# The last layer of a graph network: slice sums over normalized rows, and its weights loaded beside ELU

## The reference, cut to what matters

```python
# x: [1, 3125, 256] normalized rows; H = 8 heads, D = 64, G = 64 slices
fx_mid = (x @ W_fx + b_fx).reshape(B, N, H, D).transpose(0, 2, 1, 3)
x_mid = (x @ W_x + b_x).reshape(B, N, H, D).transpose(0, 2, 1, 3)
slice_weights = softmax((x_mid @ W_slice + b_slice) / clip(temperature, 0.1, 5.0), axis=-1)
slice_norm = slice_weights.sum(axis=2)
slice_token = einsum('bhnc,bhng->bhgc', fx_mid, slice_weights) / (slice_norm[..., None] + 1e-05)
q, k, v = slice_token @ W_q, slice_token @ W_k, slice_token @ W_v
attn = softmax(einsum('bhgc,bhkc->bhgk', q, k) * D ** -0.5, axis=-1)
out_slice = einsum('bhgk,bhkc->bhgc', attn, v)
out_x = einsum('bhgc,bhng->bhnc', out_slice, slice_weights)
return out_x.transpose(0, 2, 1, 3).reshape(B, N, 512) @ W_out + b_out
```

## Time and profile before

| | |
|---|---|
| median of 3 runs | 5513.17 us (5511.9 to 5520.0) |
| the profiled execution's own time | 5524.19 us |
| its span, first to last instruction | 5522.4 us |
| busy: PE, PEld | 4435.7 us (80%), 2884.0 us (52%) |
| busy: DVE, ACT, POOL | 3479.8 (63%), 2302.5 (42%), 3326.5 us (60%) |
| mean granted TensorE clock | 0.853 of full speed |

### The profile page before, as it was taken

How to read it: one execution, slowest core, us unless ns; L and a number is a source line. 1 busy time by engine, 2 the same in 40 slices (tenths; PEclk the granted TensorE clock), 3 DMA queues, 4 the chain that set the end, 5 groups by cost and what they waited for, 6 DMA issues and landing times. The chain is left out here.

```text
span 5522.4 us, 88485 instructions
## 1 busy us (share of the span) xinstructions
PE 4435.7 (80%) x20192; PEld 2884.0 (52%) x20192; DVE 3479.8 (63%) x12187; ACT 2302.5 (42%) x7944; POOL 3326.5 (60%) x3594
## 2 busy tenths in 40 slices
PE   6977777999867778487699968888597688878868
PEld 4533336899723335344455546666495333336536
DVE  8977884311267774624555558888524688878875
ACT  6900552333333334122555545554143455545521
POOL 7777775666477773352377747766024477758710
PEclk8966998999856668556999979999698799999978
DMA  2543346788567772132444458887475488877600
GB/s 68 161 140 104 105 103 211 251 298 292 181 187 206 206 205 40 55 104 73 116 129 130 129 133 280 281 265 207 136 212 142 118 230 232 231 209 232 182 19 24
DMA packets 528344, 914.80 MB, mean 166 GB/s; under 512 B 95861, under 2 KB 378436, under 8 KB 519396
## 3 DMA queue, kind: packets, MB, share of 16 engines
q0 software_dynamic: 154432, 449.76, 29.2%
q1 hardware_dynamic: 312974, 330.74, 19.2%
q10 hardware_dynamic: 60438, 128.64, 7.5%
HBM read 739.18 MB, written 169.60 MB: 165 GB/s over the span
## 5 line engine op out<-in xcount | busy, mean ns | idle before, releaser
L1212 PE MATMUL bank<-small 128*125 128x256 f32 x1660 | 733.8, 555 | 286.9 <-DVE small L1175 172.2
L1156 POOL DMA_INDIRECT small<-tabA,idxD x830 | 804.0, 969 | 263.9 <-issue 144.8
L1212 PEld LDWEIGHTS bank<-small 128*125 128x125 f32 x1660 | 336.4, 251 | 680.7 <-issue 361.8
L2629 POOL DMA_INDIRECT big<-tabT,edge x415 | 404.0, 973 | 247.8 <-SPq L200 121.6
L3165 POOL DMA_INDIRECT small<-tabC,idxD x415 | 408.6, 985 | 185.7 <-DVEq L202 59.4
L2903 POOL DMA_INDIRECT big<-tabB,idxD x415 | 400.2, 964 | 178.6 <-issue 86.3
L1745 DVE COPY small<-bank 128x256 f32<-128x256 f32 x176 | 74.8, 425 | 675.3 <-PE bank L1800 675.3
L1066 POOL DMA_INDIRECT eaS<-edge,rowE x391 | 393.0, 1005 | 164.7 <-issue 114.3
L1713 POOL DMA_INDIRECT small<-tabA,small x176 | 168.9, 960 | 455.5 <-SPq L200 196.5
L1187 DVE TENSOR_TENSOR big<-big,bank 125x256 f32 x830 | 346.1, 417 | 145.4 <-PE bank L1212 122.9
L3243 PE MATMUL bank<-big,cst 128*125 128x512 f32 x830 | 426.3, 595 | 0.5 <-ACT big L3230 0.5
(11 more groups left out here) (530 smaller groups left out, 10902.8 us busy)
## 6 DMA issues: line engine op xcount, KB each, us to landing
big<-in_L_w ACTq DMA_DIRECT2D x56, 1024.0 KB
small<-eaS SPq DMA_DIRECT2D x415, 128.0 KB
eaS<-small SPq DMA_DIRECT2D x415, 128.0 KB, 3.6
big<-eaS SPq DMA_DIRECT2D x415, 128.0 KB, 3.6
edge<-in_ea SPq DMA_DIRECT2D x390, 128.0 KB
big<-in_L2f_w ACTq DMA_DIRECT2D x64, 512.0 KB
big<-rowsD SPq DMA_DIRECT2D x104, 256.0 KB, 4.1
ytab<-small ACTq DMA_DIRECT2D x176, 128.0 KB
```

The lines of the kernel that those rows point to most:

```text
L1156: g.indirect_dma_start(out=self.gb[k % self.RG], out_offset=None, in_=K.tabA, in_offset=row_index(K.idxD, k)).then_inc(*self.got.up(k))
L1212: p.matmul(self.K.bank[k % 4][0:PT, 0:D], self.oh[k % self.RO][:, 0:PT], self.gb[k % self.RG], start=True, stop=True).then_inc(*self.summe ...
L2629: g.indirect_dma_start(out=self.rows(k)[:, 0, :], out_offset=None, in_=K.tabT, in_offset=row_index(K.idxS, k)).then_inc(*self.got.up(k))
```

## The change

The values are not computed tile by tile any more. PE adds the product of normalized rows (transposed by being the weights of the matmul) and slice weights over all tiles, in two banks of 128 features x 512 (head, slice) pairs. POOL adds the slice weights themselves into one tile. Behind the loop one matmul with ones sums that tile over its partitions (the norm), and 24 small ones multiply the sums with W_fx and the bias with the summed weights, which gives the tokens already transposed. DVE divides by the norm in that form, so it inverts 64 x 512 numbers. The loop's buffers change with it: the normalized rows get a ring of 7, the logits three banks, the transposes two banks.

The weight loads move in SP's order, and the fold in PE's, from behind the meeting after the ELU to before it.

```diff
+    RX = 7
...
+        self.weight, self.nr = W(512), W(512)
+        self.sums = [W(512) for _ in range(2)]
...
-    def sync(self, s):
+    def weights_sync(self, s):
...                                      (the twelve loads, as before)
+    def sync(self, s):
+        K = self.K
         K.meet(s, "s")
         K.meet(s, "s")
...
     def gpsimd(self, g):
+        w = self.weight[0:PT, :]
+        for t in range(T):
+            g.wait_ge(*self.soft.n(t + 1))
+            sv = self.sw[0:PT, t * 512:(t + 1) * 512]
+            if t == 0:
+                g.tensor_copy(w, sv).then_inc(*self.weighed.up)
+            else:
+                g.wait_ge(*self.weighed.n(t))
+                g.tensor_tensor(w, w, sv, ALU.add).then_inc(*self.weighed.up)
         self.K.meet(g, "g")
         self.K.meet(g, "g")
 
-    def tensor(self, p):
+    def fold(self, p):
...                                      (the 24 small matmuls, as before)
+    def tensor(self, p):
...
-        p.wait_ge(*self.one.n(1))
...
-                for q in range(4):
-                    m = p.matmul(K.bank[4 + q][:, 0:129], self.sw[0:PT, t * 512 + q * 128:t * 512 + (q + 1) * 128],
-                                 self.fx[t % 4][0:PT, q * 129:(q + 1) * 129], start=(t == 0), stop=(t == T - 1))
+                for c in range(2):
+                    m = p.matmul(K.bank[4 + c][:, :], self.xn[t % self.RX][0:PT, c * 128:(c + 1) * 128],
+                                 self.sw[0:PT, t * 512:(t + 1) * 512], start=(t == 0), stop=(t == T - 1))
...
-                    m = p.matmul(K.bank[1 + t % 2][0:PT, :], xT[:, c, :], self.wc[:, c * 512:(c + 1) * 512], start=(c == 0), stop=(c == 1))
+                    m = p.matmul(K.bank[1 + t % 3][0:PT, :], xT[:, c, :], self.wc[:, c * 512:(c + 1) * 512], start=(c == 0), stop=(c == 1))
                 m.then_inc(*self.logits.up)
-                if t:
-                    p.wait_ge(*self.copied.n(t))
-                for c in range(2):
-                    m = p.matmul(K.bank[3][0:PT, :], xT[:, c, :], self.wf[:, c * 512:(c + 1) * 512], start=(c == 0), stop=(c == 1))
-                m.then_inc(*self.values.up)
...
         K.meet(p, "p")
-        p.wait_ge(*self.means.n(1))
-        for q in range(4):
-            m = p.transpose(K.bank[0][0:64, q * 128:(q + 1) * 128], self.tok[:, q * 64:(q + 1) * 64], K.ident)
-        m.then_inc(*self.means_t.up)
+        p.wait_ge(*self.weighed.all)
+        p.matmul(K.bank[6][0:64, :], K.ones[0:PT, 0:64], self.weight[0:PT, :], start=True, stop=True).then_inc(*self.norm.up)
+        p.wait_ge(*self.kept_a.n(1))
+        p.wait_ge(*self.kept_v.n(1))
+        for h in range(8):
+            at = slice(h * 64, (h + 1) * 64)
+            p.matmul(K.bank[0][0:64, at], self.bf[0:PT, at], self.weight[0:PT, at], start=True, stop=False)
+            for c in range(2):
+                m = p.matmul(K.bank[0][0:64, at], self.wf[:, c * 512 + h * 64:c * 512 + h * 64 + 64], self.sums[c][:, at], start=False, stop=(c == 1))
+        m.then_inc(*self.folded_t.up)
...                                      (scalar)
         K.meet(a, "a")
+        a.activation(self.sums[0], K.bank[4][:, :], ACT.Copy).then_inc(*self.kept_a.up)
...                                      (vector)
-        for f in self.fx:
-            ins = v.memset(f.rearrange("p (q c) -> p q c", c=129)[:, :, 128:129], 1.0)
-        ins.then_inc(*self.one.up)
...
-                v.wait_ge(*self.values.n(t + 1))
-                if t >= 4:
-                    v.wait_ge(*self.slot.n(t - 3))
-                v.tensor_tensor(self.fx[t % 4][0:PT, :].rearrange("p (q c) -> p q c", c=129)[:, :, 0:128],
-                                K.bank[3][0:PT, :].rearrange("p (q c) -> p q c", c=128),
-                                self.bf[0:PT, :].rearrange("p (q c) -> p q c", c=128), ALU.add).then_inc(*self.copied.up)
...
-                if i >= 2:
-                    v.wait_ge(*self.flipped.n(i - 1))
-                ln_apply(K, v, i, self.xn[i % 2][0:PT, :]).then_inc(*self.normed.up)
+                if i >= self.RX:
+                    v.wait_ge(*self.slot.n(i - self.RX + 1))
+                ln_apply(K, v, i, self.xn[i % self.RX][0:PT, :]).then_inc(*self.normed.up)
         K.meet(v, "v")
...                                      (the division of four banks by their norm goes)
+        nr = self.nr[0:64, :]
+        v.tensor_copy(self.sums[1], K.bank[5][:, :]).then_inc(*self.kept_v.up)
+        v.wait_ge(*self.norm.n(1))
+        v.tensor_scalar(nr, K.bank[6][0:64, :], 1e-5, None, ALU.add).then_inc(*own.up)
+        v.wait_ge(*own.all)
+        v.reciprocal(nr, nr).then_inc(*self.inverse.up)
+        v.wait_ge(*self.inverse.n(1))
+        v.wait_ge(*self.folded_t.n(1))
+        v.tensor_tensor(self.tT[0:64, :], K.bank[0][0:64, :], nr, ALU.mult).then_inc(*self.tokens.up)
...                                      (tensor and sync of the whole program)
             K.meet(p, "p")
+            l3_ffn.fold(p)
             K.meet(p, "p")
             l3_ffn.tensor(p)
...
             K.meet(s, "s")
+            l3_ffn.weights_sync(s)
             K.meet(s, "s")
             l3_ffn.sync(s)
```

More of the change, by code:

```diff
@@ L3498, in __init__ @@
         keep = K.w_at
-        self.xn, self.xT = [g(D) for _ in range(2)], [g(256) for _ in range(2)]
-        self.lgt, self.fx = [g(512) for _ in range(2)], [g(4 * 129) for _ in range(4)]
+        self.xn, self.xT = [g(D) for _ in range(self.RX)], [g(256) for _ in range(2)]
+        self.lgt = [g(512) for _ in range(2)]
         self.mx, self.sm = [g(8) for _ in range(2)], [g(8) for _ in range(2)]
-        self.one = K.mark(1)
-        (self.normed, self.flipped, self.turned, self.logits, self.values, self.taken, self.copied, self.shifted, self.expo,
-         self.soft, self.slot) = (K.mark(T) for _ in range(11))
+        (self.normed, self.flipped, self.turned, self.logits, self.taken, self.shifted, self.expo,
+         self.soft, self.slot, self.weighed) = (K.mark(T) for _ in range(10))
         K.close()
         K.w_at, K.g_at = keep, 0
-        self.tok, self.nr = g(4 * 64), g(4)
         self.tT, self.qT, self.kT, self.vv, self.at, self.aT, self.oT = (g(512) for _ in range(7))
@@ L3510, in __init__ @@
         self.Bm = W(4 * D)
-        (self.means, self.means_t, self.tokens, self.qm, self.km, self.vm, self.qkv, self.scores, self.ready, self.expa, self.attn,
-         self.attn_t, self.attn_c, self.mixed, self.mixed_c) = (K.mark(1) for _ in range(15))
+        (self.norm, self.inverse, self.kept_a, self.kept_v, self.folded_t, self.tokens, self.qm, self.km, self.vm, self.qkv, self.scores, self.ready, self.expa, self.attn,
+         self.attn_t, self.attn_c, self.mixed, self.mixed_c) = (K.mark(1) for _ in range(18))
         self.back, self.back_c = K.mark(8), K.mark(8)
@@ L3579, in tensor @@
[L3579 to L3580 removed]
+                if i >= 2:
+                    p.wait_ge(*self.turned.n(i - 1))
+                p.transpose(b[:, 0:PT], self.xn[i % self.RX][0:PT, 0:128], K.ident[0:PT, 0:PT])
+                p.transpose(b[:, 128:128 + PT], self.xn[i % self.RX][0:PT, 128:256], K.ident[0:PT, 0:PT]).then_inc(*self.flipped.up)
@@ L3638, in scalar @@
                 if i >= 2:
-                    a.wait_ge(*self.values.n(i - 1))
-                a.activation(pair(self.xT[i % 2], PT), pair(K.bank[0], PT), ACT.Copy).then_inc(*self.turned.up)
+                    a.wait_ge(*self.logits.n(i - 1))
+                a.activation(pair(self.xT[i % 2], PT), pair(K.bank[7 * (i % 2)], PT), ACT.Copy).then_inc(*self.turned.up)
         K.meet(a, "a")
+        a.activation(self.sums[0], K.bank[4][:, :], ACT.Copy).then_inc(*self.kept_a.up)
         a.wait_ge(*self.ready.n(1))
```

24 lines of the change are left out of this document (5 added, 19 removed).

## The result

The changed kernel takes 5478.59 us in the median of 4 runs (5476.93 to 5486.95), the kernel before, run beside it, 5514.98 us (5511.9 to 5520.0). The ratio is 0.9936 with an interval of 0.9919 to 0.9953. The forecast was 5479.3 us. The profiled execution of the changed kernel lasted 5477.62 us with a span of 5475.8.

The account below looks back on a forecast made before the run. The prediction took DVE to bound the loop (4.87 us a tile), with preparation ahead and a dependent chain behind. Its terms, -21.7 - 1.6 - 10.6 + 0 = -33.9 us, took the median from 5513.2 to 5479.3, range 5469 to 5492.

Parts of the forecast that it names:

- A: Preparation between ELU and loop: loads and fold hidden beside the ELU, 15 us of cover left; -21.7 us.
- R4: Rival on the preparation: the cover fails and 10.5 us of fold stay exposed; -23, about 5490 us; chance 0.05.
- B: First tile of the loop: DVE no longer waits for the values before the first row sum; -1.6 us.
- C: Steady tile: dropping a DVE addition saves 0.49 us per tile, less POOL overlap of +1.2 in all; -10.6 us.
- R1: Port rival in the loop: the subtraction doubles beside POOL's addition, taking all of that gain; 5494.7 us; chance 0.08.
- D: Behind the loop, last softmax to tokens: 0 us taken, with the clock staying full; ends -3 to +3.3.
- R2: Rival behind the loop: low clock from the last slot on, +3.3 us, 5482.6 us; counted inside the forecast's 0.82.
- R3: Rival, the slower side: the loop stays at 1.2 GHz, PE needing 7.4 us per tile; 5554 us; chance 0.03.

Follow-up runs that it names:

- e1: The kernel before with only the weight loads and the fold moved beside the ELU, old loop kept: 5497.48 us, ratio 0.996 to the kernel before.
- e7: The changed kernel with three spare 512-column matmuls, results unused, on PE behind the meeting after the ELU: 5480.63 us, ratio 0.9934 to the kernel before.
- e3: The changed kernel with an unused 125x512 addition put back on DVE between the logits' addition and the maximum: 5492.86 us, ratio 0.9955 to the kernel before.
- e4: The changed kernel with POOL's addition also waiting for the next logits' addition on DVE, so starting later: 5492.56 us, ratio 0.9956 to the kernel before.
- e10: The changed kernel itself, unmodified, timed and profiled again: 5483.68 us, ratio 0.9936 to the kernel before.
- e8: The changed kernel with two more 512-column matmuls per round on PE behind the logits, results unused: 5501.61 us, ratio 0.9978 to the kernel before.

## Why the prediction was right, step by step

**A, right in size and reason.** -21.58 against -21.7. The cover was 16 us (15 forecast), the wait and DVE's own chain 0.64 + 3.43 = 4.07 against 0.5 + 3.5. R4 falls. e1 shows the term alone, without the new loop; there the first tile was 1.1 us longer than before.

**B, right.** -1.52 against -1.6. The logits came at low clock, as forecast; e7 shows that a running PE would give 2 us more.

**C, the mechanism right, the added +1.2 not needed.** The saving is 0.48 a tile and not 0.60, and e3 gives it back alone at 0.475. I had charged 0.05 per tile for the overlap of POOL and the subtraction. By the rows it is zero: POOL starts 0.77 behind L3702 (0.83 forecast) and the subtraction 0.02 later than forecast, so they miss each other by 0.01 us. R1 has no effect here, but e4 shows that 0.66 us more of delay on POOL brings it (start 1.43 behind the multiplication and not 0.77), and takes the whole gain of the loop.

**D, the step that failed.** I took the full clock behind the loop from a mean share of work, 43% per tile against 48% in another stretch. Ahead of the last slot PE idles 2.40 us in one piece, which such a share doesn't show, and on that slot the clock was low in four of the six profiles listed above. That this wait lets the clock fall is argued and not shown, since e7 and e10 have the same wait and kept the clock. From the last row sum to the tokens the term was +1.63 in the first profile and +0.11 in e10, and the remainder of the layer added 0.62 in the first and took 1.06 off in e10 (83.39 us from the tokens to the end in e10 against 84.45). So D was between -1 and +2.3 in two executions of the same kernel, within the stated -3 to +3.3, and no single value was to be had. R2's +3.3 asked for a low clock on the slot, the sum matmul and the small ones; in the first profile only the slot was slow, since the sum matmul already took 1.04 us again. It came nearer in e3, with 3.78 us for the slot and 1.94 for the sum matmul. The parts of D that rest on rows held: the reciprocal took 3.35 us (3.3 forecast), and POOL's addition was hidden. For the reciprocal the repeat count of eight in the Trainium skill, VectorE: DVE Perf Modes, section "First, the fixed hardware budget", had given an estimate of 4.3 us; the measurement decides for the rows.

**R3 falls.** The loop left the low clock after the first tile's four records, with PE idle for 20.8 us ahead of it. My argument, that the fold had not raised the clock before either, holds for the first four records and perhaps not for the next four: in e1, without the fold directly ahead, those took 2.99 us instead of 1.88, in one profile of each. That PE is the next bound is shown by e8.

**The sum.** -32.2 in the first profile and -35.5 in e10 (285.1 to 249.6), with -33.9 between them; the medians give -36.4 in the first comparison and -36.9 in e10's. That the changed kernel's median came within 0.7 us of the forecast is luck: the sizes of C and D were off by -0.7 and by +2.2 or -1.0, and the runs of the one kernel spread over 10 us. What the runs bear out is the range and the mechanism of A, B and C.

## What to carry to other kernels

An operation that leaves a chain of dependent operations saves less than its spacing, because the next one must now wait for its own input: read both spacings from the rows, the independent (0.60) and the dependent (0.72), before summing. Work moved to another engine is free only by its place in the round: list which operations of the neighbour read both their inputs from SBUF, and check that the moved one ends before them, since here 0.66 us of delay cost all that it brought. And where PE waits in single pieces, as the 20.8 us ahead of the loop and the waits of 0.8 to 4.5 us in the small attention, look at its clock behind them: matmuls whose result nobody reads, put into these waits, were worth 9 us here, most of it (8.4 of 9.8) behind the tokens.

## What the runs showed of the hardware

- A VectorE operation with two inputs in SBUF and a GpSimd addition run one after the other: 1.19 us instead of 0.69 when GpSimd (1.26) starts 0.62 us earlier; an operation with one input (e4's maximum, 0.69) or with one of its two from PSUM (the changed kernel's L3710, 0.68) keeps its time beside it.
- The reciprocal of 64x512 float32 took 3.35 us, 6.5 ns a column.
- The fold's 64x64 matmuls ran at a clock of 0.50 to their end, with PE 9.79 of 10 us busy; behind three matmuls of 128x512 (six records, 4.33 us) the next ones ran at the full clock (e7). In the kernel before, four value records behind the fold and the first logits took 1.88 us, and 2.99 where the fold was 20 us away (e1).
- With equal idle times ahead, the clock was low on the last slot in one execution of the changed kernel and not in another. What else decides it stays open.
